# Cross-attention on one core: the output projection as three rounded products, with inputs, tile order and start rearranged

## What is computed

```python
Q, K, V = split(x @ Wq.T + bq), split(ctx @ Wk.T + bk), split(ctx @ Wv.T + bv)
scores = einsum('bhqd,bhkd->bhqk', Q, K) / sqrt(32)
scores = where(mask == 0, -1e9, scores)
y = merge(einsum('bhqk,bhkd->bhqd', softmax(scores), V)) @ Wo.T + bo + x
out = (y - mean(y)) / sqrt(var(y) + 1e-5) * ln_g + ln_b
```

## Time and profile before

| | |
|---|---|
| median of 3 runs (lowest, highest) | 1701.11 us (1695.54, 1701.28) |
| the profiled execution: time, span | 1703.89 us, 1701.8 us |
| granted PE clock over the span | 0.985 of full speed |
| busy, share of the span: PE, ACT, POOL, DVE | 97%, 79%, 77%, 68% |
| DMA: share of 16 engines, rate | 66.7%, 192 GB/s |
| chain that ended last | PE 89%, DMA 3%, DVE 3%, POOL 2% |

### The profile page before, as it was taken

The page is one execution under the profiler, slowest core; times in us unless marked ns, Lnnn a source line. Parts: engine busy times, 40 slices in busy tenths (PEclk is TensorE's granted clock), DMA queues, the critical chain, the costliest instruction groups (busy, mean ns, idle before and its releaser), DMA issues.

```text
span 1701.8 us, 24832 instructions
## 1 busy us (share of the span) xinstructions
PE 1649.6 (97%) x7742; PEld 982.3 (58%) x7742; DVE 1153.7 (68%) x2835; ACT 1346.9 (79%) x1540; POOL 1303.6 (77%) x845
## 2 busy tenths in 40 slices
PE   6889999999999999999999999999999999999987
PEld 4546566565656656565665656656565665656532
DVE  7566766767676676766667676676776667677653
ACT  4388798888879788887878879887887888878673
POOL 7085787879778788878869778787877878887674
PEclk9999999999999999999999999999999999999987
DMA  7877585776767677577667668677676767756501
GB/s 251 257 211 202 161 243 175 206 200 199 204 196 217 188 203 216 169 218 208 192 179 205 203 173 241 179 203 200 191 204 204 211 185 204 217 162 187 162 8 68
DMA packets 180194, 327.51 MB, mean 192 GB/s; under 512 B 37344, under 2 KB 37344, under 8 KB 180064
## 3 DMA queue, kind: packets, MB, share of 16 engines
q1 hardware_dynamic: 180064, 325.93, 66.7%
HBM read 236.72 MB, written 89.13 MB: 191 GB/s over the span
## 4 chain that ended last, share of the span: by engine, by line
PE 89%; DMA 3%; DVE 3%; POOL 2%; issue 1%; ACT 1%; SPq 1%; POOLq 0%; DVEq 0%; ACTq 0%
PE proj_bank L969 43%; PE ctx_bank L893 14%; PE ring L862 13%; PE exp_banks L877 13%; PE ring L913 3%; DMA stack_scratch<-qk_lo 3%; PE ring L922 1%; POOL total L460 1%; DVE ring L691 1%; DVE qk_lo L719 1%; POOL c_lo L445 0%; POOL total L468 0%; PE exp_banks L987 0%; ACT qk_hi L598 0%; POOL x_lo L445 0%
## 5 line engine op out<-in xcount | busy, mean ns | idle before, releaser
L691 DVE CUSTOM_DVE_ANT_0 ring<-ring,bias 128x512 f32<-128x512 f32 x1024 | 691.2, 710 | 340.4 <-PE ring L862 340.3
L578 ACT ACTIVATE probs<-exp_banks 128x1024 f32<-128x1024 f32 x512 | 523.9, 1023 | 249.9 <-PE exp_banks L877 249.6
L552 ACT CAST exp_banks<-biasT 128x1024 f32<-128x1024 bf16 x512 | 520.7, 1017 | 25.2 <-DVE biasT L761 1.6
L877 PE MATMUL exp_banks<-q_stack,k_stack 98*128 98x512 f32 x1024 | 375.8, 449 | 3.7 <-ACT exp_banks L552 3.7
L862 PE MATMUL ring<-k_stack,q_stack 96*128 96x512 f32 x1024 | 333.3, 403 | 14.9 <-DVE maxes L691 11.9
L468 POOL TENSOR_TENSOR total<-total,probs 128x1024 f32<-128x1024 f32 x126 | 297.3, 2380 | 9.0
L460 POOL TENSOR_TENSOR total<-total,probs 128x2048 f32<-128x2048 f32 x63 | 290.0, 4603 | 10.5 <-ACT probs L578 3.9
L460 POOL TENSOR_TENSOR total<-probs 128x2048 f32<-128x2048 f32 x63 | 290.2, 4606 | 0.0
L893 PE MATMUL ctx_bank<-probs,v 128*32 128x512 f32 x2048 | 277.5, 614 | 0.7 <-DVE ctxT L752 0.7
L877 PEld LDWEIGHTS exp_banks<-q_stack,k_stack 98*128 98x128 f32 x1024 | 194.6, 191 | 107.0 <-issue 66.4
L475 POOL CAST max_parts<-maxes 128x16 fp32r<-128x16 f32 x64 | 12.5, 196 | 303.0 <-DVE maxes L691 303.0
(11 more groups left out here) (105 smaller groups left out, 1920.1 us busy)
## 6 DMA issues: line engine op xcount, KB each, us to landing
w_tile<-w_scratch SPq DMA_DIRECT2D x120, 512.0 KB, 4.6
k_stack<-stack_scratch SPq DMA_DIRECT2D x192, 256.0 KB, 5.4
q_stack<-stack_scratch SPq DMA_DIRECT2D x192, 256.0 KB, 7.1
stack_scratch<-qk_hi SPq DMA_DIRECT2D x128, 256.0 KB, 2.2
stack_scratch<-qk_lo SPq DMA_DIRECT2D x128, 256.0 KB, 2.5
raw<-cT_dram SPq DMA_DIRECT2D x64, 256.0 KB, 5.0
raw<-xT_dram SPq DMA_DIRECT2D x64, 256.0 KB, 4.9
raw<-mask_dram SPq DMA_DIRECT2D x64, 256.0 KB, 4.5
```

Of the source, the lines that this page charges most:

```text
L552: nc.scalar.copy(exp_banks[:, 2 - 2 * wave:4 - 2 * wave, :], biasT[:, kc:kc + 1, :].to_broadcast([P, 2, L])).then_inc(seeded, 1)
L578: nc.scalar.activation(probs[:, u % PS, 2 - 2 * wave:4 - 2 * wave, :], exp_banks[:, 2 - 2 * wave:4 - 2 * wave, :], ACT.Exp).then_inc(exps, 1)
L691: nc.vector.tensor_tensor_reduce(out=ring[:, n % 2], in0=ring[:, n % 2], in1=bias[:, c], scale=1.0, scalar=LOWEST, op0=ALU.subtract, op1=A ...
L877: mm = nc.tensor.matmul(exp_banks[:, h], k_stack[0:3 * D + 2, at, kc * P:(kc + 1) * P], q_stack[0:3 * D + 2, at, :], start=False, stop=Tru ...
```

## The change

- **O tiles.** `wo` becomes `wo_hi` and `wo_lo`, and the normalised context is split into `ctx_hi` and `ctx_lo`; an O tile is 12 rounded matmuls. The context is normalised into `recipT` in place, and a new `split_ctx` on DVE makes the two parts by a copy and a subtraction with all operands in SBUF. It stands at the end of a unit, one unit after the sums (three for a sequence's first group): slots 7, 9, 13 and 1. The first half of an O tile waits for two groups of its sequence, the second half for all four.
- **Inputs** land in the buffers of the low parts (`c_raw` over `c_lo`, `x_raw` over `x_lo`, the mask over `ctx_hi` and `ctx_lo`, `wo_raw` over `wo_lo`), loaded four tiles at once by `load_input`.
- **Another order of tiles** in `SLOT`, and other slots for casts, low parts and row work. Three K and Q tiles per sequence (slots 8, 9, 10) leave PSUM by DVE instead of ACT. Rows 2 and 3 of a sequence get their bias on POOL (`add_bias`) ahead of the O tile, not on DVE in PSUM.
- **The start.** One more tile ahead of unit 0; the scratch copies go to units -1 and 0, WoT and the constants to unit 1, the bias product to unit 3, the split of `wo` to units 5 (ACT) and 12 (POOL).

```diff
-    SLOT = {0: ("K", 0, 3), 1: ("Q", 0, 3), 2: ("O", -1, 0), 3: ("O", -1, 1),
...
+    SLOT = {0: ("V", 0, 3), 1: ("O", -1, 0), 2: ("O", -1, 1), 3: ("O", -1, 2), 4: ("Q", 1, 0),
...
+    BY_VECTOR = (8, 9, 10)
...
             def normalise_ctx(g):
                 dve.wait_ge(recip_wide, g + 1)
...
-                nc.vector.tensor_tensor(ctxT[:, g % CS], ctx_bank[:, 0],
-                                        recipT[:, :, :].rearrange("p a q -> p (a q)"),
-                                        ALU.mult).then_inc(normed, 1)
+                recip_all = recipT[:, :, :].rearrange("p a q -> p (a q)")
+                nc.vector.tensor_tensor(recip_all, ctx_bank[:, 0], recip_all,
+                                        ALU.mult).then_inc(normed, 1)
+
+            def split_ctx(g):
+                dve.wait_ge(normed, g + 1)
...
+                normed_ctx = recipT[:, :, :].rearrange("p a q -> p (a q)")
+                nc.vector.tensor_copy(ctx_hi[:, g % CS], normed_ctx).then_inc(ctx_rounded, 1)
+                dve.wait_ge(ctx_rounded, g + 1)
+                nc.vector.tensor_tensor(ctx_lo[:, g % CS], normed_ctx,
+                                        ctx_hi[:, g % CS].bitcast(FP32),
+                                        ALU.subtract).then_inc(ctx_split, 1)
...
+                for lag, first in ((1, False), (3, True)):
+                    if PLAN.sums(y - lag):
+                        g = PLAN.sums(y - lag)[1]
+                        if g < LAST and (g % NG == 0) == first:
+                            split_ctx(g)
...
                     if kind == "O":
-                        pe.wait_ge(normed, (seq + 1) * NG)
+                        pe.wait_ge(ctx_split, seq * NG + 2)
...
+                elif kind == "O":
+                    pe.wait_ge(ctx_split, (seq + 1) * NG)
...
                     if kind == "O":
-                        parts.append((ctxT[:, (seq * NG + t) % CS, cols], wo[:, t]))
+                        parts += output_parts(seq, n, t)
```

More of the change, by code:

```diff
@@ L78, in __init__ @@
                 kinds[tile] = len(kinds)
-        self.second_bank = [tile for tile, n in self.no.items() if n % 2 and n < 8]
+        self.second_bank = [tile for tile, n in self.no.items() if n % 2 and n < 10]
         for n in range(NC):
@@ L218, in xattn_program @@
         w_loaded = [sem(f"w_loaded{n}") for n in range(WS)]
-        raw_loaded = [sem(f"raw_loaded{n}") for n in range(RAW)]
+        in_loaded = [[sem(f"{k}_loaded{n}") for n in range(NC)] for k in ("c", "x", "mask")]
+        wo_split, row_biased = sem("wo_split"), sem("row_biased")
+        ctx_rounded, ctx_split = sem("ctx_rounded"), sem("ctx_split")
         rows_loaded = [sem(f"rows_loaded{n}") for n in range(NC)]
@@ L381, in _ @@
                         stack(tile[0], 0)
+                if PLAN.max_group(y) is not None:
+                    load_maxes(PLAN.max_group(y))
+                seq, at = y // UPS + 1, y % UPS
+                if at == 7 and 0 < seq < NB:
+                    load_input(seq, 2)
+                if PLAN.stack_group(y + 1):
+                    stack("K", PLAN.stack_group(y + 1))
                 if y == -1:
                     scratch(1, (total[:, :, :], rows[:, :, :]), wq_split, wq_scratch)
-                tile = PLAN.tile(y + 2)
@@ new lines, in _ @@
+                for tile in PLAN.rows_ahead(y, PLAN.LOADED):
+                    load_row(tile)
+                if at == 1 and 0 < seq < NB:
+                    load_input(seq, 0)
+                if at == 13 and 0 <= seq < NB - 1:
+                    load_input(seq + 1, 1)
+                if y == 1:
+                    load_weight(WoT, wo_raw[:, :, :], wo_loaded)
+                    for dst, src in ((bv_s, bv), (bo_all, bo), (g_all, ln_g), (b_all, ln_b)):
+                        sp.dma_start(dst[:, :], src).then_inc(consts_loaded, FULL)
@@ L586, in evacuate @@
                     m = seq * NC + n
-                    if m >= 5:
-                        s, kc = divmod(m - 5, NC)
+                    if m >= VS:
+                        s, kc = divmod(m - VS, NC)
                         act.wait_ge(ctx_mm, s * UPS + 3 * NC + kc + 1)
-                    nc.scalar.copy(v[:, m % 5], bank(tile)).then_inc(v_out, 1)
+                    nc.scalar.copy(v[:, m % VS], bank(tile)).then_inc(v_out, 1)
                 else:
@@ L623, in _ @@
                     tile = PLAN.tile(y - 1)
-                    if wave == 0 and tile and tile[0] != "O":
+                    if wave == 0 and tile and tile[0] != "O" and not PLAN.by_vector(tile):
                         evacuate(tile)
-                if y == -10:
-                    act.wait_ge(wk_loaded, FULL)
-                    nc.scalar.copy(by_tile(ctxT[:, 0:NG]), wk_raw).then_inc(wk_split, 1)
+                if y == -4:
                     act.wait_ge(wq_scaled, 1)
@@ L798, in _ @@
                     normalise_ctx(PLAN.sums(y)[1])
+                    if PLAN.sums(y)[1] == LAST:
+                        split_ctx(LAST)
                 if tile and tile[0] == "O":
```

323 lines of the change are left out of this document (179 added, 144 removed), and 6 rows, old and new, of the table SLOT.

## The result

| | before | after |
|---|---|---|
| median (lowest, highest) | 1700.16 us (1695.54, 1701.28) | 1904.38 us (1903.41, 1904.94) |
| ratio, 95% interval | | 1.1206 [1.1184, 1.1228] |
| profiled execution: span | 1701.8 us | 1902.3 us |
| granted PE clock over the span | 0.985 | 0.944 |
| chain that ended last | PE 89%, DVE 3%, DMA 3% | PE 63%, DVE 18%, DMA 10%, issue 7% |

Slower, as forecast (1829 us), but outside the range (1645 to 1870), on its slow side. The page's first part and the windows of the changed kernel answer to the earlier trace rows; in the windows the columns are as there.

What follows compares the result with a forecast made beforehand. PE was taken to bound the kernel, any loop wait paid in full. From the profiled 1703.9: -42.3 - 7 + 58.5 + 54.4 + 15 + 49.6 = +128.2, 1832.1; less 2.8 for the median, 1829 us; range 1645 to 1870.

Steps and rivals of the forecast that it cites:

- term 1, O tiles: Units with a rounded O tile take 5.82 us, 0.68 less; 64 of them take 43.5 us off.
- term 2, start: Ahead of unit 0, DVE's 9.84 us DMA wait goes but one more tile is computed: -7 us, bounds -12 and +5.
- slot 1, stall and clock: POOL's addition goes first and holds DVE's split; PE stalls 3.9 us, 15 times (58.5 us), plus 1.6 us of clock each.
- slot 13, stall and clock: DVE's copy first, then POOL's addition holds the subtraction; PE stalls 3.4 us, 16 times (54.4 us), plus 1.6 of clock each.
- slot 7: Split beside POOL's two half additions; slot 8's first maximum is some 1.0 us late: 15 us.
- slot 9: DVE's copy starts at the same event as POOL's small cast and wins: costs nothing.
- the tail: The last group's split, a copy and a subtraction of some 0.6 us each, stands on the chain: +1.2 us.
- Term 3: Context split on DVE and POOL's instructions exclude each other for their whole length: stalls of 58.5, 54.4 and 15 us.
- slot 13 loses both turns: POOL's additions go ahead of both copy and subtraction there, 16 x 4.6 = 74 us more: 1903 us, chance 0.12.
- Term 4: PE's clock falls to 0.55 for 3.5 us after a long stall: 31 x 1.6 = 49.6 us, bounds 0 and 50.
- at nothing: the inputs in the low parts' buffers, with one to two units between landing and cast: Loading inputs into those buffers was said to cost no time.

Runs made afterwards that it cites:

- experiments 4: Kernel before, plus an unused SBUF copy and subtraction on DVE per group at the ends of the units where the change splits: 1880.34 us, 1.1046.
- 8: Kernel before, plus the same kind of unused copy and subtraction on DVE, placed behind the second maximum of the unit after the sums: 1737.97 us, 1.0202.
- 2: Changed kernel with POOL's additions of the probabilities cut to 16 columns: 1750.61 us, 1.0284.
- 3: Kernel before with POOL's additions of the probabilities cut to 16 columns: 1691.81 us, 0.9939.
- Experiments 1: Changed kernel with the split_ctx pair moved from the unit's end to behind its second maximum, a sequence's first group a unit later: 1772.99 us, 1.0426.
- 5: Changed kernel with the split_ctx pair early, behind the second maximum, and a sequence's four masks issued one per unit in slots 7 to 10: 1716.21 us, 1.0086.
- 6: Changed kernel with only the four masks of a sequence issued one per unit in slots 7 to 10, not together in slot 7: 1886.00 us, 1.1082.
- experiments 10: On top of experiment 9: halves of K and Q tiles sent from ScalarE's DMA queue instead of SyncE's: 1767.88 us, 1.0392.
- 9: On top of experiment 5: bias of V loaded with those of Q and K, WoT and constants issued ahead of the reload of c: 1708.93 us, 1.0046.

## Why the prediction was partly right, and where it failed

| part, per the prediction | forecast | in the trace of after |
|---|---|---|
| term 1, O tiles | -43.5 | 16 x (97.9 - 100.46) = -41 |
| term 2, start | -7 | -6.0 |
| slot 1, stall and clock | 15 x 5.5 = 82.5 | 15 x (11.98 - 6.12 + 0.20 in slot 2) = 91 |
| slot 13, stall and clock | 16 x 5.0 = 80 | 15 x (4.1 + 1.4) = 83 |
| slot 7 | 15 | 15 x 1.7 = 26 |
| slot 9 | nothing | 14 x 2.3 + 5.3 = 37 |
| bias of V, unit 3 | nothing | +8.7 |

The forecast had 1.2 us more for the tail. The right column sums to +199, the spans differ by 200.5.

**Term 3 and its mechanism** held where it was worked out. Slot 1: POOL first by 0.24 us (0.3 said), PE's wait 57.8 us in 15 times, 3.85 each (3.9 said). Slot 13: the copy goes first, POOL next, and the subtraction ends 0.56 us after POOL; PE waits 2.85 us (3.4 said), fifteen times and not sixteen. That the lock is the cause is shown by experiments 4 and 8, and by 2 against 3. So the page of the Trainium skill on the two engines' shared ports (page "SBUF — State Buffer", section "Who interferes with whom") agrees with the trace: 4.58 us for a copy of 0.42.

**The rival "slot 13 loses both turns"** named 1903 us, and the result is 1904. It isn't borne out: the copy took 0.42 us in all fifteen slots 13, so only the subtraction lost its turn. The number was met by chance, with other terms.

**Term 4** took the upper end, and per stall that was right in most: 0.56 for 3.5 us in the window above, 1.5 us, and slot 14 carries 1.4 on the mean. But it isn't one price. One slot-13 stall of the fifteen, at 966 us, shows no fall behind it (interval 14 to 15 6.01 us), and behind seven of the slot-1 stalls the low clock lasts nearly twice as long, which costs 1.2 us more each. In all the clock cost some 54 us, an estimate from the intervals: 15 x 1.4 in slot 14, and for slot 1 what is left over 11.84 us without a wait and 4.0 us of stall, 8 x 1.7 and 7 x 2.8. That is a little over the upper bound of 50.

**The step that failed is "at nothing: the inputs in the low parts' buffers, with one to two units between landing and cast".** I looked at when an input lands and not at what its DMA stands in front of. The change puts six Q and K tiles in six successive units, with one buffer for the halves, and four masks beside two stacks ahead of them. Slot 9 was given "nothing" because its split wins against POOL, and it does (0.42 and 0.69 us in the slot shown): the wait there is for another thing. Experiments 1 and 5 show it, 11.78 us with the masks together and 7.03 with them spread, and 6 shows it in the changed kernel itself, 8.14 against 5.83. Term 2 had seen the same danger for the moved constants, but named the maxima of unit 4 and +5 as the bound; it was DVE's own copy in unit 3, 8.7 us, and DVE works in order, so the maxima waited behind it.

**Slot 7** was under-sized: DVE's maximum is late by the 1.0 us said (PE's recorded wait is 1.01), and the beat loses 1.7; most of the rest is a second, shorter delay: the next plain score, behind the next maximum, starts 0.65 us after the first (926.67 and 927.32 in the trace) and not 0.24.

**The range** ended at 1870 and had no bound for a transfer in it: with slot 9 at its 37 and the bias at its 9 the forecast would have been 1875. Most of the 29 us from there to 1904 are slot 7 (11), slot 1 (8.5), slot 13 (3) and a saving that came out 2.5 us smaller.

## What to carry to other kernels

Before a short instruction with all its operands in SBUF is put on VectorE, look at what GpSimd starts at the same event: where GpSimd adds 4.6 us at a time, one place costs 178 us and another, ahead of GpSimd's additions, 36, for the same work. And a stall hides others behind it: when it goes, the transfer that it covered sets the time, so look at every single buffer that a DMA must empty, at what is issued ahead of it, and at how soon what you delay is read.

## What the runs showed of the hardware that was not expected

- Behind the stall of slot 13 at 857 us the clock fell only 2.5 us after PE's work had begun again (0.93 in those 2.5 us, 0.56 in the next 3.5), so the price, 1.5 us, falls on the next unit. Behind that of slot 1 it was low almost at once (0.59 from 885.70 to 889.20 us). Equal stalls do not have an equal price: 3.85 us of waiting in each slot 1 is followed by 3.5 us of low clock in eight cases, and by some 6 us (0.50 from 996.40 to 1002.40) in seven.
- A second DMA queue did not bring the same transfers in sooner (experiments 10 and 9): 3.6 and 4.5 us from issue to landing, 3.0 and 3.9 on the busy one, though they were issued at another moment too.
- Where POOL has its next instruction ready, it goes between DVE's copy and the subtraction that depends on it: with POOL's halves of 2.4 us, 1.16 and 2.78 us for the pair in slot 7; in slot 1, where POOL's next addition waits until 890.52, the subtraction follows at once (884.95). It works the other way too: in slot 9, beside DVE's subtraction, POOL's small one at 938.33 takes 0.67 us, 0.22 at 850.62.
